# Layer 1 projects q and k in the first steps of a round and sends them from step 5 on

## The reference, cut to what matters

```python
qkv = x @ Wqkv_w.T + Wqkv_b                  # 16 heads of 16
ctx = _causal_attn(q, k, v)
ctx_c = ctx.reshape(b, s, d).transpose(0, 2, 1)
conv_out = conv(ctx_c, conv_w, padding 1) + conv_b   # three taps over the sequence
q2 = conv_out.transpose(0, 2, 1)             # as heads
ctx2 = _causal_attn(q2, k, v)                # the same k and v
out = ctx2.reshape(b, s, d) @ out_w.T + out_b
```

## The kernel before, in words

| call | kind 1 | kind 2, c 0 | kind 2, c 1 |
|---|---|---|---|
| q: part, part, high1, rest | 3, 4, 5, 6 | | |
| k: part, part, high1, rest | 6, 7, 8, 9 | | |
| fan1 of q, of k | 8, 11 | 13, 8 | 11, 6 |
| v: part, four times | 12, 14, 16, 18 | | |
| turn_c, keep_c, turn_c, keep_c | | 1, 2, 3, 4 | |
| convolve, six times | | 5 to 10 | 3 to 8 |
| high1, rest | | 11, 12 | 9, 10 |

## Time and profile before

### The profile page before, as it was taken

The page is one execution under the profiler, slowest core; times in us unless marked ns, Lnnn a source line. Parts: engine busy times, 40 slices in busy tenths (PEclk is TensorE's granted clock), DMA queues, the critical chain, the costliest instruction groups (busy, mean ns, idle before and its releaser), DMA issues.

```text
span 2138.6 us, 31862 instructions
## 1 busy us (share of the span) xinstructions
PE 1831.4 (86%) x10777; PEld 916.2 (43%) x10777; DVE 1254.6 (59%) x3777; ACT 1015.2 (47%) x2048; POOL 364.3 (17%) x555
## 2 busy tenths in 40 slices
PE   3485799999988999997479788899999999989987
PEld 2341354554434454542134344444444444544433
DVE  4545455655554444553553576767676777676663
ACT  0142456555645555565244244445454545444443
POOL 2215321221101111212443110101010100000000
PEclk8558899999999999999699899999999999999998
DMA  7236343334365444422212263545455354543430
GB/s 145 71 133 153 68 82 70 85 73 77 68 150 114 73 60 67 65 33 48 74 30 37 38 90 46 76 68 68 67 68 79 54 87 60 78 69 53 71 46 21
DMA packets 145968, 155.87 MB, mean 73 GB/s; under 512 B 26008, under 2 KB 132784, under 8 KB 145808
## 3 DMA queue, kind: packets, MB, share of 16 engines
q1 hardware_dynamic: 117728, 113.96, 33.2%
q10 hardware_dynamic: 18032, 25.44, 4.1%
q0 software_dynamic: 10048, 14.44, 3.7%
HBM read 55.95 MB, written 33.72 MB: 42 GB/s over the span
## 4 chain that ended last, share of the span: by engine, by line
PE 61%; DVE 15%; DMA 10%; issue 5%; ACTq 2%; ACT 2%; POOL 2%; SPq 2%; another core or an unknown queue 1%; DVEq 0%; POOLq 0%
PE p_PV L1018 10%; PE p_S L1001 8%; DMA t_R<-t_msp 7%; PE p_S L951 5%; PE p_S L968 4%; DVE p_S L1377 4%; PE p_Ma L1206 4%; PE p_Mb L1068 4%; PE p_S L1091 4%; ACTq L1812 2%; SPq L2134 2%; PE p_Ma L1228 2%; PE p_S L1005 1%; DVE t_mx L1363 1%; DVE t_mx L1377 1%
## 5 line engine op out<-in xcount | busy, mean ns | idle before, releaser
L1794 ACT ACTIVATE t_R<-p_S 128x512 f32<-128x512 f32 (+1 forms) x1216 | 678.3, 578 | 621.0 <-PE p_S L1005 368.9
L1377 DVE CUSTOM_DVE_ANT_0 p_S<-p_S,t_NM 128x128 f32<-128x128 f32 (+3 forms) x1024 | 483.1, 512 | 259.8 <-PE p_S L968 253.5
L1001 PE MATMUL p_S<-t_R 99*128 99x512 bf16 (+3 forms) x1536 | 479.7, 337 | 75.3 <-ACT t_R L1794 34.9
L1363 DVE TENSOR_REDUCE t_mx<-p_S 128x1 f32<-128x512 f32 x512 | 345.8, 685 | 256.2 <-PE p_S L951 234.7
L1018 PE MATMUL p_PV<-t_R 128*17 128x512 f32 (+3 forms) x3072 | 329.4, 502 | 1.1 <-ACT t_R L1794 1.0
L968 PE MATMUL p_S<-t_R 96*128 96x128 bf16 (+3 forms) x1024 | 267.1, 314 | 17.8 <-DMA t_R<-t_spl 9.3
L1001 PEld LDWEIGHTS p_S<-t_R 99*128 99x128 bf16 x1536 | 151.6, 99 | 217.0 <-ACT t_R L1794 85.0
L951 PE MATMUL p_S<-t_R 96*128 96x512 bf16 x512 | 205.8, 405 | 19.8 <-DVE t_mx L1363 19.1
L2005 POOL CAST t_spl<-t_rr 128x512 bf16<-128x512 f32 x80 | 49.7, 622 | 946.2 <-DVE t_rr L1335 946.2
L1005 PE MATMUL p_S<-t_NM 128*128 128x128 bf16 x1024 | 203.3, 224 | 0.0
L968 PEld LDWEIGHTS p_S<-t_R 96*128 96x128 bf16 x1024 | 84.6, 101 | 195.3 <-DVE t_mx L1377 88.9
(11 more groups left out here) (244 smaller groups left out, 2194.9 us busy)
## 6 DMA issues: line engine op xcount, KB each, us to landing
t_R<-t_spl SPq DMA_DIRECT2D x480, 128.0 KB
t_R<-in_w ACTq DMA_DIRECT2D x32, 512.0 KB, 9.4
t_R<-ks SPq DMA_DIRECT2D x96, 128.0 KB
ks<-t_spl SPq DMA_DIRECT2D x16, 384.0 KB, 7.8
hTd<-t_NM SPq DMA_DIRECT2D x39, 128.0 KB, 2.4
ysd<-t_NM SPq DMA_DIRECT2D x39, 128.0 KB
t_NM<-hTd SPq DMA_DIRECT2D x39, 128.0 KB, 2.5
ysd<-t_NM POOLq DMA_DIRECT2D x39, 128.0 KB, 3.1
```

The source lines that it names most:

```text
L1001: t = self.nc.tensor.matmul(bank[:, z, :], ka[0:99, h, kb * 128:(kb + 1) * 128], qa[0:99, h, n0:512], start=True, stop=not u.causal)
L1363: nc.vector.tensor_reduce(m.mx[:, g, 4 * j + qb:4 * j + qb + 1], m.S1[s1_bank(k)][:, :], AX.X, ALU.max).then_inc(s.s1_read, 1)
L1377: x = nc.vector.tensor_tensor_reduce(out=sc, in0=sc, in1=m.maskq[:, 512 - n:512], scale=1.0, scalar=NEG, op0=ALU.add, op1=ALU.max, accum_o ...
L1794: nc.scalar.activation(m.P1X[kb][j0 // per] if u.causal else m.P[p % 2][:, j0:j0 + per, :], m.s2_bank(k)[:, 0:per * n].rearrange("p (j n) ...
```

## The change

Only the order of calls in pre1 changes, and two uses of PSUM banks. For kind 1 the four half projections stand in steps 0 to 3, high1 in 2 and 4, rest in 3 and 5, fan1 in 5 (q) and 7 (k), the value projections in 10, 12, 14 and 16, and their bias in 18; q goes through Mb and k through Ma. For kind 2 with c 0 (batches 1 to 6) turn_c stands in steps 0 and 1 and keep_c in 1 and 2, the second half through Mb; two convolutions each in steps 3, 4 and 5; high1 in 6, rest in 7, fan1 of q in 9 and of k in 5. Batches 0 and 7 begin six steps later. With c 1 one convolution stands in each of steps 0 to 5, high1 in 6, rest in 7, fan1 of q in 9 and of k in 4. Units 16 and 17, prepared during the feed-forward part, start three steps earlier in their lane. The rows of maxima are issued by ScalarE's queue in both kernels.

```diff
 def bank_of(u, z):
-    return 2 if u.n < 18 else (0, 1, 0)[z]
+    return 2 if u.n < 18 else (1, 0, 0)[z]
@@ pre1
         if u.kind == 1:
-            yield from steps(3)
-            self.part(u, 0, 0)
-            yield
-            self.part(u, 0, 1)
-            yield
-            self.high1(u, 0)
-            yield
-            self.rest(u, 0)
-            self.part(u, 1, 0)
-            yield
-            self.part(u, 1, 1)
-            yield
-            self.fan1(u, 0)
-            self.high1(u, 1)
-            yield
-            self.rest(u, 1)
-            yield
-            yield
-            self.fan1(u, 1)
-            yield
+            self.part(u, 0, 0)
+            yield
+            self.part(u, 0, 1)
+            yield
+            self.high1(u, 0)
+            if u.n >= 18:
+                self.part(u, 1, 0)
+            yield
+            self.rest(u, 0)
+            if u.n < 18:
+                self.part(u, 1, 0)
+            self.part(u, 1, 1)
+            yield
+            self.high1(u, 1)
+            yield
+            self.rest(u, 1)
+            self.fan1(u, 0)
+            yield
+            yield
+            self.fan1(u, 1)
+            yield from steps(3)
             for k in range(4):
                 self.part(u, 2, k)
                 yield
                 yield
             self.values(u)
             return
-        soon = u.c or u.b not in (0, NB - 1)
-        yield from steps(3 if u.c else 1 if soon else 6)
         if u.c == 0:
-            for c in range(2):
-                self.turn_c(u, c)
-                yield
-                self.keep_c(u, c)
-                yield
+            if u.b in (0, NB - 1):
+                yield from steps(6)
+            self.turn_c(u, 0)
+            yield
+            self.keep_c(u, 0)
+            self.turn_c(u, 1)
+            yield
+            self.keep_c(u, 1)
+            yield
         for i in range(6):
             self.convolve(u, i)
-            if i == 3:
+            if i == 4:
                 self.fan1(u, 1)
-            if soon or i % 2:
+            if u.c or i % 2:
                 yield
         self.high1(u, 0)
         yield
         self.rest(u, 0)
+        yield
         yield
         self.fan1(u, 0)
@@ turn_c
-        M = self.mbank(0, s.ct_done, 2 * b + c + 1)
+        M = self.mbank(c, s.ct_done, 2 * b + c + 1)
@@ keep_c
-        self.nc.scalar.copy(m.cT[:, c, 1:513], m.MB[0][:, :]).then_inc(s.ct_done, 1)
+        self.nc.scalar.copy(m.cT[:, c, 1:513], m.MB[c][:, :]).then_inc(s.ct_done, 1)
```

## The result

| | before | after |
|---|---|---|
| median of four runs each, same chip | 2144.62 us (2140.82 to 2147.25) | 2112.53 us (2109.6 to 2116.86) |
| ratio of the times | | 0.985, 95% interval 0.983 to 0.988 |
| the profiled execution's own time | 2140.38 us | 2109.6 us |
| its span | 2138.6 us | 2107.8 us |
| mean granted TensorE clock | 0.927 | 0.938 |

The change makes the kernel faster by 32 us, 1.5%. The forecast was 2118 with a range of 2097 to 2142, and faster at 0.79. Of the 30.8 us between the two profiled executions, 28.0 lie in layer 1's rounds and 2.8 outside them. The part of the span outside them measured 1231 to 1237 us in all the kernels of this study, so 2.8 says nothing.

A forecast was written before the change was run, and what follows sets the result against it. It took TensorE's full queue, stopped chiefly by rows waits, as the bound. Terms -18 + 3 - 1.5 + 0 - 3 - 6 = -25.5 from 2140.4, plus 3.8 to the median, gave 2118 us; range 2097 to 2142.

The forecast's parts named there:

- The mechanism: Projection rounds: rows land when SyncE's fan-outs drain, so fan-outs starting 1.6 us earlier shorten TensorE's rows waits.
- Rival 1: Rows DMAs keep their own 7.8 us from issue whatever the fan-outs do: 2160 us, slower; chance 0.08.
- Rival 2: Crowded first steps of projection rounds cost 2 us instead of 0.9: 2139.5 us, no measurable change; chance 0.16.
- Rival 3: The new wait is filled and fan-outs go 3 us earlier, so all waits vanish: 2097 us; chance 0.12.
- Projection rounds: Layer 1's 14 projection rounds: of 2.2 us rows wait each, 0.9 is paid back; -18 us, bounds 0 and -30.7.
- the rows land at 26.9 - 1.6 = 25.3: In a projection round, rows land 1.6 us earlier, as the fan-outs do, at 25.3 us, when TensorE is ready.
- The price of 0.9 a round: TensorE is ready 0.9 us later in each projection round, from a new turn_o wait on Mb of about 0.95.
- The clock: Layer 1's falls to TensorE's lower clock, worth some 12 us, half come back: -6 us, bounds 0 and -12.
- First convolution rounds: In these 8 rounds, a 1.2 us stop replaces copy waits of 0.88 + 0.37: 0 us, bounds -7.5 and +6.
- Second ones: The 8 second convolution rounds: +0.35 us each, +3 in sum, while five rows waits of 0.34 vanish, -1.5.
- Step 9 waits to 12.8: Second convolution rounds: the high part (0.69 us) between exponentials 6 and 7 delays step 9; half ends near 14.8.
- Batches 0 and 7: Residue about 1.5 us earlier in units 20 and 46 cuts 9.3 us of fan-out waits: -3 us, at most -9.3.

The follow-up runs named there:

- run 3: The changed kernel, with SyncE holding q's fan-outs back until the running round's eighth exponential is done: 2144.2 us, ratio 0.999 to the kernel before.
- run 4: The changed kernel, with SyncE sending the 384 KB spill only after the rows of group 0 have landed: 2103.6 us, ratio 0.981 to before.
- run 5: The changed kernel, with q's residue of a projection round taken in step 2 and not step 3: 2106.6 us, ratio 0.982 to before.
- both: The changed kernel with q's residue a step earlier and the spill held back until the rows land: 2099.8 us, ratio 0.978 to before.
- run 8: The changed kernel with early residue, late spill, later convolutions, and an earlier residue in batches 0 and 7: 2091.8 us, ratio 0.9755 to before.
- late_fans: The kernel of run 3: the changed kernel with the fan-outs held back to near their old start, 2144.2 us.
- k1_only: The kernel before with only the new kind 1 order and its bank swap, kind 2 as before: 2119.2 us, ratio 0.988.
- k2_only: The kernel before with only the new kind 2 order, turn_c and keep_c on two banks: 2139.1 us, ratio 0.996.
- spill_late: The kernel of run 4: the changed kernel with the spill held back until group 0's rows land, 2103.6 us.
- best: The fastest kernel of the study, that of run 8, with all its edits on the changed kernel: 2091.8 us.

## Why the prediction came out right, and where its terms were off

**The mechanism held, and one size within it did not.** The rows land with the traffic of SyncE's queue (runs 3 to 5), the new order starts that traffic 2.0 us earlier (9.54 against 11.57; 1.6 were forecast), and TensorE pays 0.9 to 1.0 us a round for it (0.88 by run 3's sums, 0.96 by its parts). **Rival 1**, the rows' own latency, falls by their 7.8 us becoming 6.0, and by run 3. **Rival 2**, 2 us for the crowded steps, falls by that same price. **Rival 3**, all waits gone, did not come; it took both of the edits in `both` to get near it.

**Projection rounds: -18 forecast, -10.4 measured.** The step that failed is "the rows land at 26.9 - 1.6 = 25.3". It took the landing as the fan-outs' start plus 15.3, which would have been 9.54 + 15.3 = 24.8; 27.0 was measured. That sum holds for rows issued 6.3 us behind the start. The fan-outs moved earlier and the rows did not, so more stood ahead of them: the last two or three of K's fan-outs and the spill. Of the 2.2 us missed, 0.9 are the spill's, since without it the rows land at 26.1 (run 4). The other 1.3 are there with nothing but fan-outs ahead; that K's last ones are the cause is read from the order of the issues, and no run holds them back. The sentence "SyncE's order of issues and ScalarE's queue for the rows are as before" was true of each queue and missed their order against each other.

The term can be taken apart. Behind the projection rounds the waits for rows fall by 20.8, from the 30.7 of the prediction (the five of 0.34 lie in second convolution rounds) to 9.9; turn_o's wait costs 8.0, and TensorE's busy time at clock 1.00 is 24.06 a round where it was 23.67, 5.5 over 14. What its busy time holds above those values is 337.4 - 14 x 23.67 = 6.0 before and 340.3 - 14 x 24.06 = 3.5 after, so 2.5 is clock. -20.8 + 8.0 + 5.5 - 2.5 = -9.8, against -10.4. What the forecast missed is thus almost all in the 9.9 us of rows waits that stayed, where it had none. The price of 0.9 a round was right as a sum (13.5 in all, 0.96 each) but not in its parts: 0.6 in the wait on Mb (13 times, 0.95 was forecast 14 times) and about 0.4 in busy time, which the forecast did not have. Why the same instructions are busy longer, with modelled ends among them, stays open.

**The clock: -6 forecast, about -14 measured**, beyond the bound of -12. Again the round windows give it. The six first convolution rounds of batches 1 to 6 took 195.5 us and take 184.7. Their own order is worth 31.21 - 30.79 = 0.4 each, 2.5 in all; the remaining 8.3 are clock, as each of the six is now at 1.00. The second convolution rounds had one at 0.94 and 27.7 us in place of 26.1, worth 1.7. The rounds of batches 0 and 7, at 0.89 and 0.90 in three of four, are at 0.95 and 1.00, worth some 2.5 (TensorE's busy time there falls from 105.2 to 101.9). With the 2.5 above and about 1 lost in the last two rounds this makes 14. The forecast counted seven rounds and left out those of batches 0 and 7 and the one at 27.7; and it took half where, in the first convolution rounds, all came. Run 3 shows what the falls hang on: with the fan-outs late and the waits back, so are the falls. The size is that of one execution each, and the one profiled of after had a granted clock of 0.938 where its other three had 0.931 to 0.933, so 14 may be on the high side.

**First convolution rounds: 0 forecast, -2.5 by their own order.** The waits at the copies were sized nearly right (1.0 us for 1.2). Of the 0.42 a round only 0.13 is less idle time: `out` no longer waits for q's residue at line 1228 (1.6 us in six waits before), and turn_f's new wait at line 891 takes 0.4 a round. The other 0.29 is TensorE's busy time at clock 1.00, 29.56 before and 29.27 after; why it is shorter stays open, as in the projection rounds. **Second ones: +3 - 1.5 forecast, -1.9 measured** beside the clock, 26.07 to 25.76 in each. "Step 9 waits to 12.8" did not come: the order of high1 ahead of exponential 7 costs nothing that the rounds show, and the 0.34 of the rows went. **Batches 0 and 7: -3 forecast, -4.0 measured**, but by another way: 2.5 of it is clock, and the fan-out waits fall from 9.3 to 8.3 only, as q's residue stays behind step 13's split in DVE's queue. Taken a step earlier (run 8), the waits are 1.3.

**In sum:** the projection rounds came 10 us short of the forecast without their clock (-7.9 for -18), the clock gave 8 more, the orders of the convolution rounds 4 more (-2.5, -1.9 and -1.5 where 0, +1.5 and -3 stood), and what lies outside the rounds 3 more. -25.5 + 10 - 8 - 4 - 3 makes the -30.8 of the profiled executions, to the rounding. That the total came within 6 us of the forecast is luck in this sense: an error of 10 us one way stood against errors of 15 the other.

**Not tried:** the old banks with the new order. Mb for k would make turn_o wait for k's residue, which stands behind turn_o's own division in DVE's queue, so neither would start. A kernel that changes the clock alone is not to be had; run 3 comes nearest.

## What to carry to other kernels

A small DMA that the critical path waited for landed with the bulk traffic issued ahead of it, though that was on another engine's queue; so when bulk transfers move, put the issues of all queues in one order of time and look at what now stands ahead of the small one. Move or hold back what nobody waits for (here one wait ahead of a 384 KB spill was worth 9 us). When waits of 2 us go from an engine that is 86% busy, count the clock falls in the dense rounds behind them too, in every kind of round: here they gave more (14 us) than the waits less their price (22.5 - 8.0 - 5.5 = 9.0).

## What the runs showed of the hardware that was not expected

The granted clock in a round whose instructions do not change goes with what the rounds before it waited for: in `late_fans` four first convolution rounds of six are at 0.95 and 32.2 to 32.3 us, in after all six at 1.00 and 30.8, and in `k1_only` five of six are at 1.00 and 31.2, with the code that took 32.6 to 33.7 at 0.95 and 0.90 in the kernel before.

Windows of 1 us over rounds 4 to 27 (counted from 0; they hold the convolution rounds of batches 1 to 6) show where the clock goes to 0.50. The kernel before has eight such falls, and seven of them begin within 1.5 us of the start of a round that had waited 1.9 to 2.6 us for rows. `late_fans` has seven, all behind waits of 1.7 to 2.8 us, and `k2_only` ten, all behind waits of 1.8 to 2.7. After has two, one of them behind a wait (1.8 us). `spill_late`, where no such wait is over 1.0 us, has one, and `best` none. The round of the kernel before that began behind a wait of 2.53 us, in two windows:

```profile
1584.52:1589.52 5.00, 5.00 (x35) 2.39 (x36) 2.66 (x15) 2.24 (x5) 0.00 (x0) 0.66 0.00 1
1589.52:1612.63 23.11, 20.00 (x161) 10.79 (x159) 17.59 (x65) 11.33 (x23) 3.54 (x4) 1.00 0.66 88
```

Not each wait brings a fall: the rounds of before that began at 1473.85 and 1500.35 had waited 2.80 and 2.15 us and stayed at 1.00. And no run here has the waits without the late fan-outs, so the two are not told apart.

A spread of that kind also makes single profiles of this kernel uncertain by some 3 us: the projection rounds of after held two at 0.94 (like that at 1573.49), those of `k1_only` none behind the first, so its sum is the smaller one, 364.4 against 368.0, with the same code there.
